# A decoder layer on one core: all key and query stacks loaded on SyncE's queue, turned tokens copied ahead of rotated sums on ScalarE, output bias of the second batch later, another pace for the middle

## The reference, cut to what matters

```python
x = x + attn(layernorm(x), w_qkv, b_qkv, w_o, b_o)      # 32 query heads, 8 key/value heads of 32, rotary, causal
x = x + xattn(layernorm(x), ctx)                        # fake_quant(x1) @ fake_quant(x2)
x = x + ffn(layernorm(x), W_org, lora_down, lora_up, lora_keys, Wq)

def attn(x, ...):
    q, k, v = split(x @ w_qkv.T + b_qkv)
    q, k = apply_rope(q), apply_rope(k)
    scores = where(causal, q @ k.T / sqrt(32), -1e20)   # four query heads share one key/value head
    return softmax(scores) @ v @ w_o.T + b_o

def ffn(x, ...):
    base = x @ W_org.T
    coeffs = softmax(scores of the mean token)          # weights of 8 experts of rank 64
    return base + sum_e coeffs[e] * (x @ lora_down[e]) @ lora_up[e]
```

## Time and profile before

| | kernel before |
|---|---|
| median of three runs | 702.71 us |
| the profiled execution, its own time | 701.59 us |
| span of the profiled execution, first to last instruction | 699.8 us |
| mean granted TensorE clock | 0.985 |
| busy: TensorE | 651.6 us (93%) |
| busy: VectorE, ScalarE, GpSimd | 427.6, 423.0, 283.2 us |
| loads issued by GpSimd | 33, with 15.73 MB |

### The profile page before, as it was taken

One profiled execution on the slowest core, in us unless ns is written; L12 is line 12 of the kernel. 1 busy time (PEld: TensorE's weight loads), 2 busy tenths in 40 slices (PEclk: granted clock), 3 DMA queues, 4 the chain that ended last, 5 costly groups with the idle time before them and its releaser, 6 DMA issues.

```text
span 699.8 us, 12690 instructions
## 1 busy us (share of the span) xinstructions
PE 651.6 (93%) x4512; PEld 527.5 (75%) x4512; DVE 427.6 (61%) x1127; ACT 423.0 (60%) x1025; POOL 283.2 (40%) x317
## 2 busy tenths in 40 slices
PE   4996899999999899999889799899999999899998
PEld 3985677888877678888666577688777778688886
DVE  6795777876877734665886965533144899821122
ACT  5425678878778847679968685756233793720310
POOL 2047645534444263347320540515634205943520
PEclk9999999999999999999997989999999999999999
DMA  7648854752455523323663341313434363433102
GB/s 261 241 140 243 237 143 127 218 147 76 140 152 172 174 103 110 121 58 95 181 183 123 87 119 30 112 40 89 153 120 143 129 204 128 152 123 103 46 25 95
DMA packets 43934, 93.47 MB, mean 134 GB/s; under 512 B 5504, under 2 KB 5888, under 8 KB 42432
## 3 DMA queue, kind: packets, MB, share of 16 engines
q1 hardware_dynamic: 34416, 66.45, 29.4%
q0 software_dynamic: 3696, 15.73, 9.4%
q10 hardware_dynamic: 5760, 10.49, 4.1%
HBM read 72.72 MB, written 19.92 MB: 132 GB/s over the span
## 4 chain that ended last, share of the span: by engine, by line
PE 68%; DVE 12%; ACT 7%; issue 5%; POOL 5%; DMA 2%; ACTq 0%; DVEq 0%
PE dense L1092 33%; PE score L1092 8%; PE probt L980 8%; PE pv L996 5%; PE score L968 5%; PE pv L1092 3%; POOL w_lo L1715 2%; ACT prob_all L1186 2%; DVE stats L1389 2%; DVE xres L1493 2%; ACT w_hi L1139 1%; PE misc L1005 1%; DVE prob_all L1344 1%; DVE w_lo L1324 1%; PE misc L1035 1%
## 5 line engine op out<-in xcount | busy, mean ns | idle before, releaser
L1344 DVE CUSTOM_DVE_ANT_0 prob_all<-score,mask_sb 128x128 f32<-128x128 f32 (+3 forms) x256 | 123.2, 488 | 115.9 <-PE score L968 114.3
L1715 POOL TENSOR_TENSOR w_lo<-stage,w_hi 128x512 fp32r<-128x512 f32 x85 | 109.9, 1302 | 194.7 <-ACT w_hi L1139 194.3
L1092 PE MATMUL dense<-w_hi,act_t 128*128 128x512 f32 (+1 forms) x536 | 180.1, 390 | 7.5 <-POOL w_lo L1715 2.5
L1186 ACT ACTIVATE prob_all<-prob_all,neg_max 128x128 f32<-128x128 f32 (+3 forms) x256 | 142.7, 558 | 36.6 <-DVE neg_max L1344 34.9
L1092 PE MATMUL dense<-act_t,w_hi 128*128 128x512 f32 x366 | 123.2, 418 | 1.3 <-POOL w_lo L1715 1.2
L980 PE MATMUL probt<-ident_sb,prob_all 128*128 128x128 f32 x640 | 115.0, 279 | 5.6 <-ACT prob_all L1195 3.5
L1092 PEld LDWEIGHTS dense<-w_hi,act_t 128*128 128x128 f32 x536 | 100.2, 193 | 24.6 <-POOL w_lo L1715 4.5
L1092 PE MATMUL dense<-w_lo,act_t 128*128 128x512 f32 (+1 forms) x298 | 107.6, 379 | 0.7 <-ACT w_lo L1144 0.3
L980 PEld LDWEIGHTS probt<-ident_sb,prob_all 128*128 128x128 f32 x640 | 80.2, 143 | 24.7 <-issue 9.3
L1139 ACT ACTIVATE w_hi<-stage 128x512 fp32r<-128x512 f32 x117 | 72.1, 623 | 44.0 <-PE dense L1092 18.4
L1195 ACT ACTIVATE prob_all<-probt 128x128 f32<-128x128 f32 (+3 forms) x160 | 68.6, 429 | 48.2 <-PE probt L980 46.7
(11 more groups left out here) (204 smaller groups left out, 1011.1 us busy)
## 6 DMA issues: line engine op xcount, KB each, us to landing
q_stack<-rope_dram POOLq DMA_DIRECT2D x15, 768.0 KB, 7.1
stage<-in_w_qk SPq DMA_DIRECT2D x40, 256.0 KB, 2.9
rope_dram<-act_t ACTq DMA_DIRECT2D x40, 256.0 KB, 2.8
stage<-in_w_o SPq DMA_DIRECT2D x32, 256.0 KB, 2.9
stage<-in_ctx_kv SPq DMA_DIRECT2D x24, 256.0 KB, 3.3
stage<-in_w_org SPq DMA_DIRECT2D x24, 256.0 KB, 3.3
xres<-in_x SPq DMA_DIRECT2D x8, 512.0 KB, 5.9
prob_all<-in_x SPq DMA_DIRECT2D x8, 512.0 KB, 6.2
```

The costliest lines, as they stand in the source:

```text
L1092: last = engine.matmul(dst, lhs, rhs, start=(k == 0 and c == 0), stop=(k == g.kts - 1 and c == len(pairs) - 1))
L1186: engine.activation(prob[:, u % P_SLOTS, 0:length], prob[:, u % P_SLOTS, 0:length], ACT.Exp, bias=neg_max[:, m:m + 1], scale=-1.0, accum_o ...
L1344: engine.tensor_tensor_reduce(prob[:, u % P_SLOTS, 0:length], score_bank[u % 2][:, 0:length], mask_sb[:, S - length:S], -1.0, HIGHEST, ALU ...
L1715: engine.tensor_tensor(slot_lo(p, 0, NW), raw_of(p), slot_hi(p, 0, NW).bitcast(F32), ALU.subtract).then_inc(g_piece, 1)
```

## The change

It has five parts. (1) `load_stacks`, `load_first_keys` and `load_first_queries` move from GpSimd's program to SyncE's, with the same slots, waits and bytes; in a slot they stand behind `put_roped` and ahead of the fetches. Their destination is named as float32 in place of fp32r. (2) On ScalarE, for slots with u < 0, `rope_high` stands behind the turned tokens' copy (`tokens_high`) and not ahead of it; for u >= 0 nothing changes. (3) The output bias of batch 1 is added for tile i not before the slot in which `out` 1 begins that tile, plus 4. (4) The pace of the cross steps is 1.6 in place of 1.15, and (5) the pace of `base` 0 is 1.1 in place of 1.15.

```diff
-    PACES = [(("out", 0, 0), 0.55), (("down", 0, 0), 1.15), (("out", 1, 0), 1.0)]
+    PACES = [(("out", 0, 0), 0.55), (("cross", 0, 0), 1.15), (("base", 0, 0), 1.6), (("down", 0, 0), 1.1), (("out", 1, 0), 1.0)]
@@ sync_program @@
+            def load_stacks(gi):
+                b, g = divmod(gi, NKV)
+                mk, mq = plan.rope_no["k", b, g // GROUP], plan.rope_no["q", b, g]
+                if gi >= 2:
+                    e.wait_ge(t_score, last_unit(gi - 2) + 1)
+                e.wait_ge(*roped(mk))
...
+                engine.dma_start(k_stack[0:TERMS * HD, gi % 2, :].bitcast(F32), rows).then_inc(d_kstack[gi % 2], 16)
+                e.wait_ge(*roped(mq))
...
+                engine.dma_start(q_stack[0:TERMS * HD, gi % 2, :, :].rearrange("p h c -> p (h c)").bitcast(F32),
+                                 rows).then_inc(d_qstack[gi % 2], 16)
...
                 for m in rope_out_at.get(j, ()):
                     put_roped(m)
+                if j == first_queries_at:
+                    load_first_keys()
+                    for pair in range(GROUP // 2):
+                        load_first_queries(pair)
+                for gi in load_at.get(j, ()):
+                    load_stacks(gi)
                 for p in at["fetch"].get(j, ()):
                     fetch(p)
@@ scalar_program @@
-                for m in rope_high_at.get(j, ()):
-                    rope_high(m)
+                if u >= 0:
+                    for m in rope_high_at.get(j, ()):
+                        rope_high(m)
...
                 for halves in at["turn"].get(j, ()):
                     tokens_high(*halves)
+                if u < 0:
+                    for m in rope_high_at.get(j, ()):
+                        rope_high(m)
@@ gpsimd_program @@
-                if j == first_queries_at:
-                    load_first_keys()
-                    for pair in range(GROUP // 2):
-                        load_first_queries(pair)
-                for gi in load_at.get(j, ()):
-                    load_stacks(gi)
...
-                if NT <= biased < B * NT and u >= UNITS + 8 + 2 * (biased - NT):
+                if NT <= biased < B * NT and u >= UNITS + 8 and j >= plan.slot_of[plan.begin["out", 1, 0, biased - NT]] + 4:
                     add_output_bias(1, biased - NT)
```

More of the change, by code:

```diff
@@ L796, in load_second, with load_first_keys, load_first_queries @@
                 engine.dma_start(x_second[:, t, :], x[1, t * P:(t + 1) * P, :]).then_inc(d_xb[t], 16)
+            def load_stacks(gi):
[4 more added lines that the diff above has]
+                e.wait_ge(*roped(mk))
+                rows = rope_dram[mk].rearrange("a (r h) c -> h r a c", h=GROUP)[g % GROUP]
+                engine.dma_start(k_stack[0:TERMS * HD, gi % 2, :].bitcast(F32), rows).then_inc(d_kstack[gi % 2], 16)
+                e.wait_ge(*roped(mq))
+                rows = rope_dram[mq].rearrange("a (r h) c -> r a (h c)", h=GROUP)
+                engine.dma_start(q_stack[0:TERMS * HD, gi % 2, :, :].rearrange("p h c -> p (h c)").bitcast(F32),
+                                 rows).then_inc(d_qstack[gi % 2], 16)
+            def load_first_keys():
+                m = plan.rope_no["k", 0, 0]
+                e.wait_ge(*roped(m))
+                rows = rope_dram[m].rearrange("a (r h) c -> h r a c", h=GROUP)[0]
+                engine.dma_start(k_stack[0:TERMS * HD, 0, :].bitcast(F32), rows).then_inc(d_kstack[0], 16)
+            def load_first_queries(pair):
+                m, heads = plan.rope_no["q", 0, 0], slice(2 * pair, 2 * pair + 2)
+                e.wait_ge(*roped(m))
+                rows = rope_dram[m].rearrange("a (r h) c -> r a h c", h=GROUP)[:, :, heads, :].rearrange("r a h c -> r a (h c)")
+                engine.dma_start(q_stack[0:TERMS * HD, 0, heads, :].rearrange("p h c -> p (h c)").bitcast(F32),
+                                 rows).then_inc(d_qfirst[pair], 16)
             def fetch(p):
@@ L1670, in rope_low @@
                 engine.tensor_tensor(r["raw"].bitcast(F32R), r["raw"], r["high"].bitcast(F32), ALU.subtract).then_inc(g_rlo, 1)
[L1672 to L1696, removed]
             def ln(instruction):
```

## The result

The changed kernel takes **698.7 us** (median of 6 runs, 697.8 to 700.1) against 702.96 for the kernel before in the same comparison (6 runs, one of them an outlier of 1273.95 us): a ratio of 0.9935, 95% interval 0.9909 to 0.9960, so 4.6 us less, somewhere between 2.8 and 6.4. The forecast was 700.6 us with a range of 695.5 to 705.0: the sign and the range held, the gain was about twice the 2.1 us of the sum. The profiled execution took 698.77 us with a span of 697.0, 2.8 less than before.

What follows compares the result with a forecast made beforehand. TensorE was taken to bound the kernel, with only its idle time and slow stretches to win. Terms -1.67 + 0.3 - 0.7 = -2.1 us turned 702.71 into 700.6 us, range 695.5 to 705.0.

Steps and rivals of the forecast that it cites:

- What bounds the kernel: Whole kernel: TensorE, busy 651.6 of 699.8 us, sets the time; only its 48 us idle and slow stretches can be won.
- Part 1, the loads leave GpSimd: Head: without the loads on GpSimd, `add_sine` of job 3 and the chain behind it come 1.67 us earlier; nothing in the units.
- The loads on SyncE: Queue effect of the moved loads on themselves and fetches behind them, notably in the cross stage: 0, between -1.0 and +3.7 us.
- The estimate from time for each MB: Stack loads: GpSimd's queue 67 us of an engine per MB, SyncE's 50, so a 0.96 MB load lands 1.0 us sooner.
- Part 2, the turned tokens first: Head, u = -8: the 3.10 us stall goes, but its gain is waited for again behind u = 0; 0 of its own.
- Part 3, the bias: GpSimd's output bias: tiles 0 to 2 hide in idle time, tile 3 delays a low rest; costs 0.3 us, 0 to 2.4.
- Part 4, the cross pace: Cross stage: steps shift between slots, but the start of `base` 0 at 218 stays; no change in time.
- the middle speeds up too: Rival, cross stage: the clock stays up in one stretch, 4.1 us more won, 696.5 us; chance 0.32 together with both head stalls.
- Part 5, the base pace: Base stage: steps come later than pieces, shrinking TensorE's 1.78 us wait at 453.33; gain 0.7 us, 0 to 1.8.
- The clock: TensorE's clock: left as it is, no reason seen for a change in either direction.
- nothing is won: Rival, head: group 0's stacks land 1.67 us later from SyncE's queue and the first score waits; 702.3 us, chance 0.14.
- The slower middle: Rival, cross stage: lower clock lasts half as long again, losing 4.1 us, and fetches lose 3.7; 708.4 us, chance 0.12.

Runs made afterwards that it cites:

- the second execution: The changed kernel run once more without edits, against the kernel before in a second comparison: 699.42 us, ratio 0.9926.
- job 4 moved: Changed kernel with ScalarE's high part of job 4 also behind the tokens' copy: 696.75 us, ratio 0.9922; with the output bias load seven slots later too: 697.77 us, 0.9901.
- the two profiles with that load moved away: Batch 1's output bias load issued seven slots later: in the kernel before, 702.98 us, 0.9992; in the changed kernel with job 4 moved, 697.77 us, 0.9901.

## Why the prediction was right, and where it wasn't

**What bounds the kernel** held: all that was won was idle time or time at the lower clock on TensorE, whose busy time went from 651.6 to 651.0 us.

**Part 1, the loads leave GpSimd (-1.67).** `add_sine` of job 3 starts 1.44 us earlier, and the loads alone bring the first score 1.9 us forward. The term was right for the head. It was wrong to carry it to the end: at unit 8 nothing is left of it with the loads alone, and the time is that of before (1.0001). The step that failed is "from u = 8 on all runs 1.7 us ahead"; what the profiles say of its cause is under the clock.

**The loads on SyncE (0, bounds -1.0 to +3.7)** held. Nothing waits behind them in the cross stage, where the upper bound was put:

```profile
359.32 0.60 SPq L808 DMA_DIRECT2D q_stack<-rope_dram  x1
...
365.07 1.56 SPq L830 DMA_DIRECT2D stage<-in_ctx_kv  x2
```

The fetch is issued at 365.07, before at 365.08, and of 23 pieces fetched from 335 to 415 us the slowest landed after 4.9 us (5.0 before). A `q_stack` lands after 6.8 us (median of 15) against 7.1. The estimate from time for each MB, 1 us sooner, had no ground: q1's share grew by as much as q0's had been. The Trainium skill, page "DMA: Bandwidth & Descriptors", section "Issuing engines are not separate DMA queues", has transfers run on the same engines whichever engine issues them, and only the issue time saved; the traces agree, with 38.8% before and 38.3% after.

**Part 2, the turned tokens first (0 beyond part 1)** held in size, and the mechanism in part: alone it takes 2.26 us off the first stall, puts 1.21 onto the second (1.50 to 2.71) and leaves the time at 0.9990. In the changed kernel the second stall is 2.56 us.

**Part 3, the bias (+0.3, 0 to 2.4).** Right in kind, and near in size: some 0.5 us. Three of the four instructions stand back to back in the gap that was named, and the fourth came after two low rests:

```profile
513.35 7.55 POOL L1742 TENSOR_TENSOR prob_all<-prob_all,xnorm 128x1024 f32<-128x1024 f32 x3
527.46 3.00 POOL L1725 TENSOR_TENSOR w_lo<-stage,w_hi 128x512 fp32r<-128x512 f32 x2 [6.56 <-ACT w_hi L1171]
530.42 2.85 POOL L1742 TENSOR_TENSOR prob_all<-prob_all,xnorm 128x1024 f32<-128x1024 f32 x1
```

**Part 4, the cross pace (0).** Too low. By slots the plan hardly changes, and from that the prediction took no change in time. The column from unit 128 to step 400 holds 1.2 us more or less for a stretch near 245 us that lasts 3.4 or 6.8 us, whatever the kernel; with that evened out it is +0.4 us on average for the six kernels with the new pace and -0.4 for the eight with the old one. So about 0.8 us, with a scatter as large, and nothing that its own run's ratio shows (0.9993, 0.9965 to 1.0021). The stalls there are no fewer (a new one of 1.53 us stands at 360), but less time is spent at the lower clock. If it is real, it is the first rival, "the middle speeds up too", at a fifth of its price of 4.1 us.

**Part 5, the base pace (-0.7, 0 to 1.8).** This is the term that was mis-sized. It is worth 2.7 us by its ratio (1.1 to 4.3). The prediction took one wait, the one for the low rest at 453.33, and there were three, 1.54 + 0.74 + 1.16 = 3.4 us, all for a `w_lo` that GpSimd had just made. The one that it took is the least certain: it goes with the late landing, without any change of pace. The two that it didn't look at are in every profile with the old pace, and the slower pace takes them from 1.9 down to 0.5 us. That is 1.4 of the 1.9 us that the column from step 400 to 448 shows for the pace; the rest has no row of its own. Whether the pace also takes the first wait when the piece lands late, no run shows. The upper bound of 1.8 was that one row. Reading TensorE's waits in the window of the whole stage would have shown the sum.

**The clock (0).** Not 0 in the head, though whether the change brings it isn't shown. Of the changed kernel's 2.47 us, the longer second stall takes 2.56 - 1.50 = 1.06, and 3.4 us at the lower clock about another. The price of that clock is best read where it is largest: the kernel with both paces alone trails by 4.2 us at unit 16 after 13.6 us at 1.2 GHz, 0.3 us for each; the loads alone lose 1.8 us between units 4 and 8 with 6.8 us there, about as much. So 1.0 us here, and 2.47 - 1.06 - 1.0 = 0.4 is left; 0.8 was seen at unit 8 and 0.15 at unit 64. In the second execution 1.4 at the first score, less 0.3 of stall and 1.0 of clock, is 0.1, and 0.3 was seen. The Trainium skill, page "TensorE: Matmul & The Clock Gate", section "Terms", puts the penalty at half the time that is spent at the half rate; by it 13.6 us would cost 6.8, and the timelines show 4.2. TensorE was busy 24.3 of the 30 us around it, so some of the slower work may have run where it would have waited; that is argued, not shown.

**The sum.** What lasts of head and bias is about 0 (0.9995 for the two, with an interval of 1.7 us to either side), of the paces -4.6 (0.9935, or -3.5 by the medians), and -4.6 was measured. The forecast had -1.4 for the first and -0.7 for the second: the sign and the range held, partly by luck, since two thirds of the forecast gain came from a term that didn't last, and a larger one than was forecast stood in for it. The rival "nothing is won" was right about the head by another mechanism than its own, since the one wait for `q_stack` at the first scores, with the old paces, is 0.22 us. The slower middle didn't come: in the two stretches that the prediction counted it is 13.7 us (17.1 before), between the 11 and 22 that it had set, and with the one near 245 us 17.1 (20.5 before). The chances gave faster by over 0.5% a third; the ratio says 0.65%, and its interval (0.40 to 0.91%) leaves the case "within 0.5%" possible too.

**What stays open:** why the piece behind the output bias lands 2 us later in three profiles and not in the others, and whether the 1.5 us wait that it makes is there in most executions, since five kernels whose profile lacks it are no faster (ratios 0.9990 to 1.0001); whether the slower pace takes that wait too; what lets the clock fall in the head, and whether the change has a part in it; and whether the head's lead with job 4 moved reaches the end, for which 1.65 us between two medians speak, but not the intervals.

## What to carry to other kernels

Before pricing a change of pace or order, add up all waits of the bounding engine for the same producer over the whole stage, not the one row that caught the eye: here three short waits for one kind of operand stood where one was priced, and a pace 4% lower took two of them from 1.9 to 0.5 us. Before calling a wait a property of the kernel, look for it in several profiles: the longest of the three was in three of eight. A stall that is moved from ahead of a chain to behind it wins nothing until the next link of the chain is moved too; ask which instruction of the same kind comes next, here job 4 behind job 3. A lead early in a kernel has to be followed to the end, event by event, before it is called a gain. And before a change is blamed for a slow stretch, check that the stretch begins behind the first instruction that differs.

## What the runs showed of the hardware that wasn't expected

The same work in the head ran at 2.4 GHz throughout in six profiles of seven with the old order and fell to 1.2 GHz for 13.6 us in the seventh; the middle had 13.7 to 23.9 us at the lower level. In the head of that seventh profile a microsecond at 1.2 GHz cost 0.3 us, with TensorE busy 24.3 of the 30 us around it. With a changed head, four profiles of seven fell to 1.2 GHz at 58.7 to 59.4 us, ahead of every instruction that had moved. A 256 KB piece fetched right behind a 512 KB load on the same queue landed after 3.8 to 4.6 us or after 5.9 to 6.2, and after 2.9 and 3.0 us in the two profiles with that load moved away. Issuing a stack load costs SyncE's queue 0.60 us (median of 15) where GpSimd's took 0.56.
